# Attention and two local-attention layers on one core: query norm multiplied in on GpSimd, a third of the gate product there, and another beginning

## What is computed

```python
def ref_attn(x):      # 16 heads of 8 features
    Q, K, V = proj(Wq, bq), proj(Wk, bk), proj(Wv, bv)    # reshaped n, s, h, d
    attn = softmax(einsum('nqhd,nkhd->nhqk', Q, K) * 8 ** -0.5)
    return attn_out @ Wo.T + bo
def layer(x):         # twice; 8 heads of 64, window 64
    q, k, v = split(shift_token(x) @ wqkv)
    q, k = rotary_xpos(l2norm(q) * qs, l2norm(k) * ksc)
    x = x + local_attention(q * 8, k, v) @ wo     # own window and the one before, causal
    a, g = split((layernorm(shift_token(x)) * lg + lb) @ w1 + b1)
    return x + (a * gelu(g)) @ w2 + b2
out = x + ref_attn(layernorm(x)) + layer(layer(layernorm(x)))
```

## Time and profile before

| | |
|---|---|
| median of 3 runs | 1637.84 us (1637.82 to 1640.18) |
| profiled execution | 1640.42 us, its span 1638.6 us |
| ACT busy | 1472.9 us, 90% |
| PE busy | 1384.8 us, 85% |
| DVE busy | 1342.5 us, 82% |
| POOL busy | 1237.4 us, 76% |
| granted TensorE clock, mean | 0.969 |

### The profile page before, as it was taken

One profiled execution on the slowest core, in us unless ns is written; L12 is line 12 of the kernel. 1 busy time (PEld: TensorE's weight loads), 2 busy tenths in 40 slices (PEclk: granted clock), 3 DMA queues, 4 the chain that ended last, 5 costly groups with the idle time before them and its releaser, 6 DMA issues.

```text
span 1638.6 us, 40224 instructions
## 1 busy us (share of the span) xinstructions
PE 1384.8 (85%) x14680; PEld 1099.8 (67%) x14680; DVE 1342.5 (82%) x2149; ACT 1472.9 (90%) x4176; POOL 1237.4 (76%) x1607
## 2 busy tenths in 40 slices
PE   1578789998989989898989989998998988688885
PEld 1366577777777767777777767777777776577664
DVE  4998899898989989898888989898888686558731
ACT  1468799999999999999999999999999999598993
POOL 2758788787888888888888888788878784577741
PEclk9788899999999999999999999999999999899998
DMA  5021012221211122221211122121211211111120
GB/s 153 10 42 39 11 35 48 47 46 36 59 34 40 31 48 47 41 51 32 60 34 37 33 48 47 41 47 35 61 32 34 39 40 39 19 27 34 22 54 21
DMA packets 177637, 67.82 MB, mean 41 GB/s; under 512 B 146933, under 2 KB 152354, under 8 KB 177442
## 3 DMA queue, kind: packets, MB, share of 16 engines
q1 hardware_dynamic: 176146, 64.70, 18.7%
q10 hardware_dynamic: 1296, 0.56, 0.1%
HBM read 17.54 MB, written 8.39 MB: 16 GB/s over the span
## 4 chain that ended last, share of the span: by engine, by line
ACT 70%; PE 10%; issue 9%; DVE 5%; POOL 3%; DMA 1%; SPq 1%; ACTq 0%; DVEq 0%; POOLq 0%
ACT sb_pl L644 24%; ACT sb_pl L651 10%; ACT sb_pT L597 5%; ACT sb_sq L621 4%; ACT sb_kT L597 3%; ACT sb_oTl L597 3%; ACT sb_hid L684 3%; ACT sb_v L597 3%; ACT sb_hn L667 3%; ACT sb_qT L597 3%; PE banks L983 2%; ACT L679 2%; ACT L644 2%; ACT sb_gate L679 2%; PE banks L972 2%
## 5 line engine op out<-in xcount | busy, mean ns | idle before, releaser
L644 ACT ACTIVATE sb_pl<-banks,sb_nml,sb_rn 128x128 f32<-128x128 f32 x1024 | 466.0, 515 | 5.2 <-POOL sb_nml L577 4.8
L554 POOL TENSOR_TENSOR sb_qk<-sb_qk,sb_t 128x1024 f32<-128x1024 f32 x128 | 304.8, 2381 | 47.4 <-DVE sb_t L813 47.4
L549 POOL TENSOR_TENSOR sb_pr<-sb_qkvf 128x2048 f32<-128x2048 f32 x64 | 291.8, 4559 | 3.7 <-DVE sb_qkvf L767 3.7
L644 ACT ACTIVATION_READ_ACCUMULATOR sb_pl<-banks,sb_nml,sb_rn 128x1 f32 x1024 | 268.7, 262 | 0.0
L651 ACT ACTIVATE sb_pl<-sb_pl,sb_rl 128x128 f32<-128x128 f32 x640 | 213.1, 459 | 0.2 <-DVE sb_rl L833 0.2
L883 PE MATMUL banks<-sb_wqh,sb_hh 128*128 128x512 f32 x384 | 175.7, 458 | 43.6 <-DVE sb_t L813 34.5
L828 DVE TENSOR_REDUCE sb_nmx<-banks 128x4 f32<-128x512 f32 x256 | 164.1, 683 | 42.2 <-PE banks L961 42.1
L972 PE MATMUL banks<-sb_ident,sb_pl 128*128 128x128 f32 x1024 | 162.3, 283 | 27.7 <-ACT sb_kT L597 10.5
L621 ACT ACTIVATE sb_sq<-banks 128x1024 f32<-128x1024 f32 x128 | 137.3, 1073 | 44.1 <-PE banks L885 44.1
L597 ACT ACTIVATE sb_pT<-banks 128x512 f32<-128x512 f32 x256 | 165.8, 672 | 4.6 <-PE banks L972 4.5
L808 DVE TENSOR_TENSOR sb_qk<-banks,sb_tab 128x1024 f32<-128x1024 f32 x128 | 154.9, 1210 | 12.7 <-ACT sb_sq L621 12.6
(11 more groups left out here) (120 smaller groups left out, 3698.2 us busy)
## 6 DMA issues: line engine op xcount, KB each, us to landing
sb_vs<-sb_v SPq DMA_DIRECT2D x224, 128.0 KB, 2.4
sb_xt<-x SPq DMA_DIRECT2D x16, 256.0 KB, 3.0
heads_scratch<-sb_ofs SPq DMA_DIRECT2D x64, 64.0 KB, 3.3
sb_orow<-heads_scratch SPq DMA_DIRECT2D x16, 256.0 KB, 2.9
sb_ob<-x SPq DMA_DIRECT2D x16, 256.0 KB, 2.9
out<-sb_ob SPq DMA_DIRECT2D x16, 256.0 KB, 3.4
sb_hh<-sb_sh SPq DMA_DIRECT2D x16, 128.0 KB, 2.4
sb_hl<-sb_sl SPq DMA_DIRECT2D x16, 128.0 KB, 2.4
```

What stands on the lines that cost most here:

```text
L549: nc.gpsimd.tensor_tensor(pr[:].rearrange("p (q k d) -> p q k d", q=H, k=H), q[:, :, None, :].to_broadcast([P, H, H, D]), k[:, None, :, :] ...
L554: nc.gpsimd.tensor_tensor(qk[:, k, :], qk[:, k, :], t2[:, TURN[step] % 2, :], ALU.add).then_inc(s_add.sem, 1)
L644: last = nc.scalar.activation(pl[:, k, m, :], ps[:, m * P:(m + 1) * P], ACT.Exp, bias=nml[:, k, m:m + 1], scale=rn[:, TURN[step] // 2 % RN ...
```

## The change

1. Query and key are both multiplied by their norms in "normed" on POOL, 128x1024. "row_scale" and its buffer go, the row maximum is the exponential's bias as it is, and the exponential has no scale. It waits for its own half of "row_max" instead of for the row scaling of both.
2. Of the three gate products of a unit the first two are done on DVE in one instruction that adds the bias to the up half in PSUM and multiplies by the gate ("hid"). Their copies on ACT go. The last third is as before, now called "pool_hid" (POOL_HID = 1).
3. POOL_SCALED is (2, 6): POOL scales two groups of eight, ACT six.
4. The beginning: a semaphore for each kind of load; ACT loads only the identity, and runs a dummy exponential before its first step; SP issues x, layer 0's weights, the tables and the projection weights, and the rest ("weights", five steps) lies in the step order. The rotation table is loaded once; POOL writes layer 1's scaled table and then scales layer 0's in place. The high half of layer 1's weights, the gain and the high half of the up weights are made on ACT ("high_q", "gain", "high_up").
5. All places are new, and the first and last units have a scale each besides (FIRST_SCALE 0.94 to 1.05, LAST_SCALE 0.47 to 0.97).

```diff
-POOL_SCALED = (1, 4, 6)
+POOL_HID = 1
+POOL_SCALED = (2, 6)
...
-LAST_AT = (-5.0039757, -2.9663610, -1.9718764, -0.5737843, 0.4163776)
+LAST_AT = (-4.8382878, -2.9062629, -0.9651967, -1.1040628, 0.1136649)
+LAST_SCALE = (0.9670584, 0.7425029, 0.4668260, 0.7402405, 0.6229305)
...
+            sp.dma_start(wq_rows[0], t["wqkv"][0]).then_inc(s_wq, 16)
+            for dst, src in table_loads:
+                sp.dma_start(dst, src).then_inc(s_rows, 16)
+            for dst, src in first_loads:
+                sp.dma_start(dst, src).then_inc(s_wx, 16)
             for step in STEPS:
                 kind, s, l, n = step
+                if kind == "weights" and n == 0:
+                    sp.wait_ge(s_wq, 16)
+                    sp.dma_start(identb[:], t["c_identb"]).then_inc(s_mask.sem, 16)
+                    sp.dma_start(mask[:, :, :], t["c_mask"]).then_inc(s_mask.sem, 16)
+                    sp.dma_start(wq_rows[1], t["wqkv"][1]).then_inc(s_w1.sem, 16)
...
+                if kind == "tables":
+                    layer = 1 - n
+                    pool.wait_ge(s_rows, 16 * len(table_loads))
+                    nc.gpsimd.tensor_tensor(part, raw, rows, ALU.mult).then_inc(s_tab.sem, 1)
...
-                    nc.gpsimd.tensor_tensor(k3, k3, rn[:, TURN[step] % RNS, LH:2 * LH, None].to_broadcast([P, LH, LD]), ALU.mult).then_inc(s_nrm.sem, 1)
-                if kind == "hid":
+                    nc.gpsimd.tensor_tensor(both, both, rn[:, TURN[step] % RNS, :, None].to_broadcast([P, 2 * LH, LD]), ALU.mult).then_inc(s_nrm.sem, 1)
+                if kind == "pool_hid":
...
-            for dst, src in first_loads:
-                act.dma_start(dst, src, allow_slow_non_contiguous=True).then_inc(s_wx, 16)
+            act.dma_start(ident[:], t["c_ident"]).then_inc(s_id, 16)
             act.wait_ge(s_const, 3)
+            nc.scalar.activation(rs2[:, 0:1], half[:, 0:1], ACT.Exp)
...
-                    act.wait_ge(s_nml.sem, s_nml.at(same("row_scale", step, n // 2), step))
+                    act.wait_ge(s_max.sem, s_max.at(same("row_max", step, n // 2), step, n % 2 + 1))
                     for m in range(4):
                         last = nc.scalar.activation(pl[:, k, m, :], ps[:, m * P:(m + 1) * P], ACT.Exp, bias=nml[:, k, m:m + 1],
-                                                    scale=rn[:, TURN[step] // 2 % RNS, 2 * m + n % 2:2 * m + n % 2 + 1], accum_out=suml[:, k, m:m + 1])
+                                                    accum_out=suml[:, k, m:m + 1])
...
+                if kind == "hid":
+                    dve.wait_ge(s_up.sem, s_up.at(same("up", step, n), step, 2))
+                    dve.wait_ge(s_gelu.sem, s_gelu.at(same("gelu", step, n), step))
+                    nc.vector.scalar_tensor_tensor(hid[rows, n, :], bank(same("up", step, n), 1)[rows, :], b1[rows, l, 0, n:n + 1], gates,
+                                                   ALU.add, ALU.mult).then_inc(s_hid.sem, 1)
```

More of the change, by code:

```diff
@@ L45 @@
 LAST_HEADS = (B - 2, B - 1)
-HEADS_AT = (0.3413570, 0.4991559, 3.8117712, -4.4646283, -0.4851747)
-HEADS_SCALE = (0.5958681, 1.1193597, 0.7838495, 1.0049087, 1.0274403)
+HEADS_AT = (0.4634402, 0.7559115, 2.5889320, -4.5843117, -1.7930715)
+HEADS_SCALE = (0.6122646, 0.9697668, 1.0901495, 0.9335650, 0.7285575)
 UNIT_SLOTS = {
[L51 to L68, removed]
@@ L307, in build @@
         s_w3 = signal("w3_split", "split_w3", 2)
-        s_wqs = signal("wqkv_split", "split_q", 2)
+        s_wqh = signal("wqkv_high", "high_q")
+        s_wqs = [signal(f"wqkv_split_{k}", "split_q", 2 - k, only=lambda step, k=k: step[3] == k) for k in range(2)]
         s_tab = signal("tables_scaled", "tables")
@@ L437, in build @@
+        assert tuple(len(part) for part in loads) == OTHER_LOADS
         block = ctx.enter_context(nc.Block())
@@ L675, in _ @@
                         act.wait_ge(s_bias.sem, s_bias.at(("biases", 0, 0, 0), step))
+                        act.wait_ge(s_tab.sem, s_tab.at(("tables", 0, 0, 1), step))
                     if before(step, 2):
-                        act.wait_ge(s_hid.sem, s_hid.at(("hid", *before(step, 2)[1:]), step))
+                        done, last = gated(before(step, 2))
+                        act.wait_ge(done.sem, done.at(last, step))
                     rows = hidden_rows(n)
@@ L680, in _ @@
                 if kind == "up_copy":
-                    act.wait_ge(s_up.sem, s_up.at(same("up", step, n), step, 2))
+                    part = HT - POOL_HID + n
+                    act.wait_ge(s_up.sem, s_up.at(same("up", step, part), step, 2))
                     in_order(same("gelu", step, 0), step)
-                    rows = hidden_rows(n)
-                    nc.scalar.activation(hid[rows, n, :], bank(same("up", step, n), 1)[rows, :], ACT.Identity, bias=b1[rows, l, 0, n:n + 1]).then_inc(s_upc.sem, 1)
+                    rows = hidden_rows(part)
+                    nc.scalar.activation(hid[rows, part, :], bank(same("up", step, part), 1)[rows, :], ACT.Identity, bias=b1[rows, l, 0, part:part + 1]).then_inc(s_upc.sem, 1)
                 if kind == "x1_split":
@@ L732, in _ @@
[L732 to L736 removed]
+                if kind == "split_q" and n == 0:
+                    dve.wait_ge(s_wq, 16)
+                    split(wqh[:, 0, :], wql[:, 0, :], wq_rows[0], s_wqs[0], step)
@@ L742, in _ @@
                 if kind == "biases":
-                    in_order(("tables", 0, 0, 1), step)
                     dve.wait_ge(s_fold.sem, s_fold.at(("fold", 0, 0, 0), step))
@@ L899, in _ @@
                     claim(step)
-                    pe.wait_ge(s_w, 16 * len(loads))
+                    pe.wait_ge(s_w.sem, s_w.at(("weights", 0, 0, 4), step))
                     for k in range(2 * DEPTH * HT):
@@ L952, in _ @@
                     kb = TURN["q_copy", s, l, n] % 2
+                    if s == 0 and l == 0 and n == 0:
+                        pe.wait_ge(s_mask.sem, s_mask.at(("weights", 0, 0, 0), step))
                     for h in range(2):
```

203 lines of the change are left out of this document (114 added, 89 removed).

## The result

| | before | after |
|---|---|---|
| median | 1638.24 us (1637.82 to 1640.18) | **1532.88 us** (1530.59 to 1533.38) |
| ratio | | **0.9352**, 95% [0.9336, 0.9368] |
| profiled execution, span | 1640.42, 1638.6 | 1533.33, 1531.5 us |
| ACT / PE / DVE / POOL busy | 1472.9 / 1384.8 / 1342.5 / 1237.4 | 1377.1 / 1364.1 / 1368.3 / 1215.8 |
| granted TensorE clock, mean | 0.969 | 0.969 |

The account below looks back on a forecast made before the run. The prediction took ACT alone to set the steady-state pace, with latencies at both ends. From the profiled 1640.4 us, -54 steady state, -12 start and -9 tail gave 1565, stated as 1564 us against the median; range 1530 to 1608.

Parts of the forecast that it names:

- Exponentials, 0.09 us each: Steady state on ACT: dropping the second per-row operand saves 0.09 us per exponential, 5.9 us per sample.
- costs what it did: Rival, steady state: the exponential gets no shorter, ACT stays at 91.6 us per sample, 1626 us; chance 7%.
- Leader's share, 97%: Steady state: ACT, the fullest engine, is busy 97% of a sample, so 88.3 us per sample, 4.1 less.
- fits nearly perfectly: Rival, steady state: the order lets ACT reach 99%, 86.5 us per sample, 1537 us in total; chance 14%.
- three full engines hold each other up: Rival, steady state: ACT reaches 94% or less as margins shrink, 1602 us or more; chance 14%.
- Start: Beginning: earlier second x and first transpose move the first query projection to about 21 us; -12 us, bounds -5 and -20.
- the 28 us that I had named as refutation: Start: the forecast counts as wrong if the first query projection stays beyond 28 us.
- the subtraction's 4.2 us: Start: DVE's layer 1 subtraction held beside a POOL product; the 4.2 us can stay, inside the bounds.
- the two waits that I had named: Start: first transpose waits for ACT's nine loads until 17.87 us; second x, behind 32 DMAs, is issued at 22.90.
- the lock rival: Rival, steady state: each new DVE step waits for POOL's instruction in flight, 4 us per sample, 1613 us; chance 4%.
- Tail: From 1400 us on: shorter exponentials -8, row scaling and copies -1, spacing unpriced; -9 us, bounds 0 and -20.
- The slower rival: Rival, steady state: PE, and ACT behind it, waits for POOL's longer norm, 94.1 us per sample, 1649 us; chance 4%.

Follow-up runs that it names:

- experiment 6: Changed kernel with each DVE gate product followed by a like instruction that writes over the up half in PSUM; 1550.49 us, ratio 0.9441.
- experiment 8: Changed kernel with each matmul that writes the mask into a scores bank done twice on PE; 1552.62 us, ratio 0.9457.
- experiment 2: Kernel before, exponentials without their per-row scale, POOL multiplying row maxima by ones, query norm left out of local scores; 1559.07 us, ratio 0.9509.
- experiment 5: Changed kernel with POOL taking a third group of probabilities again, POOL_SCALED (1, 4, 6), places unchanged; 1580.91 us, ratio 0.963.
- experiment 7: Kernel before with part 2 of the change alone, two of three gate products on DVE, in the old order; 1658.47 us, ratio 1.0096.
- experiment 4: Changed kernel with two POOL waits added at the beginning, tables and first product each after a DVE weight split; 1529.66 us, ratio 0.9331.
- experiment 9: Changed kernel with POOL's table scalings behind the first product, which waits for DVE's split of layer 0's weights; 1527.68 us, ratio 0.9319.
- experiment 11: Changed kernel with PE waiting for all first loads before its first transpose; 1534.45 us, ratio 0.9358.
- experiment 12: Changed kernel with all weight loads issued by SP ahead of the second sample; 1545.22 us, ratio 0.9429.
- experiment 3: Changed kernel with part 1 undone: POOL norms keys only and scales row maxima, the exponential has its scale; 1649.06 us, ratio 1.0054.
- experiment 1: Changed kernel with a per-row operand of ones given to every exponential as scale; 1617.73 us, ratio 0.9862.
- experiment 10: Changed kernel with a third group of probabilities on POOL, POOL_SCALED (2, 4, 6); 1546.32 us, ratio 0.9435.

## Why the prediction was right, and where not

*Exponentials, 0.09 us each: right.* 0.34 for 0.44 in the row, 84.9 us when a column of ones is put back, 79 us (1638.2 to 1559.1) when it alone is taken from the kernel before. The rival "costs what it did" is dead. The Trainium skill (ScalarE: Activation LUTs, "What ACT_TABLE_LOAD costs") gives about 93 ns for each per-row pointer operand; the runs agree, also for an exponential with a row sum behind it.

*The other sizes per sample.* ACT 85.3 (forecast 85.7), DVE 83.7 (85.3), PE 83.1 (84.2), POOL 75.2 (77). POOL's norm was under its bounds: I took twice the 512 norm, 2 x 1.05, and 1.92 is the price. A fixed part of about 0.18 us, paid once instead of twice, would fit the two means; that is an estimate, no run separates it.

*Leader's share, 97%: the mis-sized term.* It was 98.5%, and the period of 86.6 is that of the rival "fits nearly perfectly" (86.5), to which I had given 14%. 85.3 / 0.97 would be 87.9, it is 86.6: 1.3 us a sample, and with the 0.4 us of ACT's work, that is the forecast's 88.3 - 1.7. That makes 22 of the 31 us by which I was off. I argued from DVE's 96% at the start and ACT's 96.5% while filling, two stretches with latencies of their own; experiments 6 and 8 show that this order has slack: 2.6 or 3.7 us more on a neighbour cost 0.44 and 0.31 of themselves. The neighbours also stood lower than I had them, 1.6 and 2.2 us below ACT instead of 0.4 and 1.5: I took their busy time of a 92.5 us sample as fixed work. In experiment 2, with the same instructions on DVE and PE but one sample in 86.63 us, it is less: 753.45 and 758.48 of 800 us, so 81.6 and 82.1 us a sample where I had counted 82.5 and 84.15. But the rival "three full engines hold each other up" is no invention. Experiments 5 and 7 take work off ACT without new places for the rest, and both lose.

*Start: -15.6 for -12, by the wrong steps.* The statistics came at the forecast 13 partly by luck: I had the second x issued at 10 us and 3.1 us on its way, and it was issued at 7.00 and took 5.75. (33 DMAs stood ahead of it before, where I had counted 32.) The query projection was at 30.19 and so beyond the 28 that I had named as refutation. The step that failed is the lock at the start: I priced the subtraction's 4.2 us "inside the bounds", and did not price POOL's tables at all beside DVE's casts (2.11 for 0.33, 2.58 for 0.56 us). The runs of experiments 4 and 9 take them apart. That the size of the start came out near the forecast is luck: the projection came 2.9 us earlier and not 12. Of the two waits that I had named, the one on all first loads is worth nothing measurable (experiment 11) and the load order 10.6 us (experiment 12); 1.0 is the operand's (experiment 2), and the other 4 stay open. The gain shows in DVE's work: DVE is busy 48.0 of the first 60 us, where it was 37.6, and 89.5 of 100 to 200 us for 84.0, so its queue seems to be further along when the late projection comes.

The rule of the Trainium skill (SBUF — State Buffer, "Who interferes with whom") names casts too, by their two-port mode, and I had applied it to the subtractions alone; 2.11 against 0.33 us agrees with it. It was also right on the new step of DVE with one tensor in PSUM: 0.74 us, none of it held, so the lock rival does not occur in the steady state.

*Tail: -15.6 for -9.* The exponentials gave 5.3 in experiment 2 (forecast 8). The other 10.3 I had at 1 for the row scaling and 0 for the spacing. How they divide between the two no run separates. Experiment 3 shows ACT standing 8.9 us for the row scaling from 1200 us on, and a tail 20 us longer than that of experiment 1, so its way over POOL may be a large share of them.

*The slower rival* (PE waits for POOL's norm): not in the change, 5.3 us in 128 steps where there had been 11.7, but it is the wait that appears in experiments 5 and 10 when POOL gets one group more.

*The sum.* 54, 12 and 9 off the median 1637.84 are 1563, not 1564; I slipped by 1 us.
